# Products without a reader on TensorE, ahead of the first queries and beside the 24 leading maxima

## The chip, the cores and the metric

The kernel runs on one core of one Trainium2 chip. The metric is the time of one execution on the device in microseconds (us), median of the runs; a profiled execution gives the trace that the views are read from. Its span runs from the first to the last instruction, so it is a little shorter than the time.

## The reference, cut to what matters

Two transformer layers over `x` of shape (4, 512, 128). Each normalizes `x`, and adds attention with 16 heads of 8 dimensions and a feed-forward part, both taken from the same normalized `x`:

```python
xn = _layernorm(x)
x = x + _L0_attn_ref(xn, ...) + _L0_ffn_ref(xn, ...)
xn = _layernorm(x)
x = x + _L1_attn_ref(xn, ...) + _L1_ffn_ref(xn, ...)   # block mask; 8 experts, top 2
...
scores = jnp.einsum('bhqd,bhkd->bhqk', q, k) / math.sqrt(HEAD_DIM)
attn = jax.nn.softmax(scores, axis=-1)                 # needs the largest score of each row
out = jnp.einsum('bhqk,bhkd->bhqd', attn, v)
```

The change touches neither inputs nor outputs of any of this.

## The kernel before

The work is cut into eight units (`U = 8`), one for each layer and sequence. A unit has 32 pairs of heads and query tiles for the maxima and 16 slots for the rest of the attention. The order on each engine is written out by hand in five programs, one for each engine, which meet at semaphores.

**The start.** SyncE loads `xs` and the first weights. VectorE takes the statistics, GpSimd the deviation, VectorE normalizes (`normalize`, L521). TensorE turns the result over in `xnT_mms` (four f32 transposes, L729), ScalarE copies it to SBUF (`xnT_copy`, L1003), and TensorE makes queries and keys in `qk_mm` (L735: w_q and w_k, f32, 512 columns; a product is two instructions in the trace) and values in `v_mms` (L741). ScalarE copies with bias (L1020) and, with VectorE, splits each value into three bf16 parts (L1008, L573, L1013, L577). SyncE writes the parts to DRAM (`z`, L422) and reads them back in the layout of the operands `QO` and `KO` (L443).

**The leading maxima.** Ahead of unit 0, 24 pairs of its maxima are made (`LEAD = 24`). `max_mms` (L777) issues two bf16 products of 48 rows by 512 columns for each pair; one works on partitions 0 to 47, the other on 64 to 111. They fill one of three pairs of PSUM banks (banks 0 to 5), and `read_max` on VectorE (L1194) reduces 1,024 columns to the maxima. `take_pair` makes a pair of banks wait for the read that last used it, three jobs back in a list `taken`. After 20 pairs stand four small transposes (`max_transposes`, L784), of which ScalarE makes `mT` (L1027), and two DMAs put it into rows of `QO` (L470).

**The slots.** In `tensor_unit` each slot has two pairs of score products (L792), two pairs of maxima for later (L777), eight instructions of `value_mms` (L808, f32, into bank 6, `PV_BANK`), and side work. ScalarE takes the exponential of each score pair (L1034).

Bank 6 is used at the start for the queries of unit 0 and then for the bias of the values (`value_bias`, L755), which VectorE reads in `add_value_bias` (L1183), with `v_bias_added` as its signal. After that nobody touches it until `value_mms` of slot 0.

Of the kernel before, what the change touches and what calls it, by code (L numbers as in the profile page):

```python
# [12 lines left out]
P = 128  # L13
# [4 lines left out]
def build(nc, x, wq, wk, wv, bq, bk, bv, wo, bo, wg_T, wu_T, wd_T, src_blocks, tgt_blocks, router_T, eg_T, eu_T,  # L18
# [3 lines left out]
    NT = S // P  # L22
# [19 lines left out]
    PROD_ROWS, MASK_ROW, M_ROW, ROWS = 48, 48, 56, 59  # L42
# [9 lines left out]
    with ExitStack() as ctx:  # L52
        def sb(name, shape, dt=F32):
            return ctx.enter_context(nc.sbuf_tensor(name, shape, dt))

        def sem(name):
            return ctx.enter_context(nc.semaphore(name))

        ident = sb("ident", [P, P])
# [44 lines left out]
        QO = [sb(f"QO{i}", [P, H // 2, S], BF16) for i in range(3)]  # L104
        KO = [sb(f"KO{i}", [P, H // 2, S], BF16) for i in range(3)]
# [50 lines left out]
        ps = ctx.enter_context(nc.psum_tensor("ps", [P, 8, 512], F32))  # L156
# [5 lines left out]
        PV_BANK, SIDE = 6, 7  # L162
# [23 lines left out]
        v_bias_added = sem("v_bias_added")  # L186
# [72 lines left out]
        def layer(u):  # L259
            return u // B  # L260
# [12 lines left out]
        def rows_of(t, half, j, rows, blocks):  # L273

            return t[64 * half:64 * half + rows, j, blocks[0] * P:blocks[1] * P]

        def reads_of(u):

            return 16 * sum(4 if layer(v) == 0 else 16 for v in range(u % 3, u + 1, 3))

        def late_reads_of(u):

            return 16 * 16 * sum(layer(v) == 1 for v in range(u % 3, u + 1, 3))
# [50 lines left out]
        def take_pair(pe, kind, n):  # L334

            i = turn[kind, n]
            if i >= 3:
                before, m = taken[i - 3]
                left = {"score": exp_done, "max": max_read, "gate0": h_ready[0], "gate1": h_ready[1],
                        "places": places_ready, "expert": y_copied}[before]  # L340
                pe.wait_ge(left, m + 1)
            return i % 3
# [383 lines left out]
        def xnT_mms(pe, p, bank):  # L726
            pe.wait_ge(xn_ready, p + 1)
            for t in range(NT):
                last = pe.transpose(ps[:, bank, t * P:(t + 1) * P], xe[p % 2][:, t, 0, 0:D], ident[:])  # L729
            last.then_inc(xnT_ps, 1)  # L730

        def qk_mm(pe, p, side, bank):
            pe.wait_ge(xnT_ready, p + 1)
            w = (w_q, w_k)[side][layer(p)]
            pe.matmul(ps[:, bank, :], w[:], xnT[p % 4][:], start=True, stop=True).then_inc(qk_ps, 1)  # L735

        def v_mms(pe, p, bank):
            if layer(p) == 0:
                for t in range(NT):
                    tok = slice(t * P, (t + 1) * P)  # L740
                    last = pe.matmul(ps[:, bank, tok], xnT[p % 4][:, tok], w_v[0][:], start=True, stop=True)  # L741
            else:

                for h in range(H):
                    for c4 in range(4):
                        last = pe.matmul(ps[32 * c4:32 * c4 + 32, bank, 32 * h:32 * h + 32],
                                         xnT[p % 4][:, 32 * h:32 * h + 32], w_v[1][:, 32 * c4:32 * c4 + 32],
                                         start=True, stop=True)
            last.then_inc(v_ps, 1)

        def value_bias(pe):

            pe.wait_ge(proj_loaded, 16 * 3)
            pe.wait_ge(part_ready[0], 1)
            pe.matmul(ps[:, PV_BANK, 0:D], b_v0[:].to_broadcast([P, P]), w_proj[0][:], start=True, stop=True).then_inc(  # L755
                v_bias_ps, 1)

        def max_mms(pe, q):
            u, m = q // PAIRS_U, q % PAIRS_U
            s, qt, jj = m // 8, m % 8 // 2, m % 2  # L760
            if m == 0:
                if u == 0:
                    pe.wait_ge(first_rows[0], 16 * 4)
                else:
                    pe.wait_ge(qk_rows[u % 3], reads_of(u))
                if B <= u < B + 3:
                    pe.wait_ge(mask_rows, 32 * (u - B + 1))
            if q == PAIRS_U // 4:
                pe.wait_ge(first_rows[1], 16 * 4)
            if q == PAIRS_U // 2:  # L770
                pe.wait_ge(qk_rows[0], reads_of(0))
            if m == PAIRS_U // 2 and layer(u) == 1:
                pe.wait_ge(late_rows[u % 3], late_reads_of(u))
            pair = take_pair(pe, "max", q)
            rows = PROD_ROWS if layer(u) == 0 else M_ROW
            for half in range(2):
                mm = pe.matmul(ps[:, 2 * pair + half, :], rows_of(QO[u % 3], half, 2 * s + jj, rows, (qt, qt + 1)),  # L777
                               rows_of(KO[u % 3], half, 2 * s + jj, rows, (0, NT)), start=True, stop=True)
            mm.then_inc(max_ps, 1)

        def max_transposes(pe, u, a):
            pe.wait_ge(m_split, 2 * u + a + 1)
            for t in range(NT):
                last = pe.transpose(ps_bf(SIDE)[0:24, t * P:(t + 1) * P],  # L784
                                    mp[:, a, t].rearrange("p h i j -> p (h i j)"), ident_bf[:])
            last.then_inc(mT_ps, 1)
# [103 lines left out]
        def side_mms(pe, u, slot):  # L890

            w, n, p, f = u - 1, u + 1, u + 2, u + 3
            if slot == 0 and 1 <= u and p < U:
                pe.wait_ge(mT_ready, 2 * u + 1)
                pe.wait_ge(h_ready[0], GATES_U * min(u, B))
                qk_mm(pe, p, 0, SIDE)
# [8 lines left out]
            if slot == 2 and u == 0:  # L905
                qk_mm(pe, p, 0, SIDE)
            if slot == 3 and u >= 1:
                normalized_transposes(pe, w)
            if slot == 4 and p < U:
                pe.wait_ge(qk_f_ready, 2 * p + 1)  # L910
                pe.wait_ge(onT_ready, u)
                qk_mm(pe, p, 1, SIDE)
# [75 lines left out]
        def last_tensor(pe):  # L988
            u = U - 1
            value_mms(pe, SLOTS_U * U - 1)  # L990
            pe.wait_ge(on_ready, 2 * u + 1)
            out_transposes(pe, u, 1)
            normalized_transposes(pe, u)

            out_mms(pe, u, (0, 1), PV_BANK)
            pe.wait_ge(onT_ready, u + 2)
            out_mms(pe, u, (2, 3), PV_BANK)
# [432 lines left out]
        @block.sync  # L1430
        def _(sp):
            load_x(sp, 0)
            for dst, src in first_loads:
                sp.dma_start(dst, src).then_inc(first_loaded, 16)
            load_x(sp, 1)
            load_x(sp, 2)
            for dst, src in proj_loads:
                sp.dma_start(dst, src).then_inc(proj_loaded, 16)
            operand_writes(sp, 0, 0)
            operand_writes(sp, 0, 1)  # L1440
            first_reads(sp)
            row_constants(sp, 0)
            for dst, src in ffn_loads:
                sp.dma_start(dst, src).then_inc(ffn_loaded, 16)
            operand_writes(sp, 1, 0)
            operand_writes(sp, 1, 1)
            operand_reads_0(sp, 1)
            max_rows(sp, 0, 0)
            row_constants(sp, 1)
            row_constants(sp, 2)  # L1450
            load_x(sp, 3)
            for dst, src in loads:
                sp.dma_start(dst, src).then_inc(loaded, 16)
            for u in range(U):
                sync_unit(sp, u)
            for b in ARRIVALS:
                load_results(sp, b)
            for b in ARRIVALS:
                store(sp, b)
            sp.wait_ge(stored, 16 * B)  # L1460
# [65 lines left out]
        @block.tensor  # L1526
        def _(pe):
            pe.wait_ge(consts, N_IDENT)
            xnT_mms(pe, 0, SIDE)
            pe.wait_ge(first_ready, 1)  # L1530
            qk_mm(pe, 0, 0, PV_BANK)
            qk_mm(pe, 0, 1, 4)
            v_mms(pe, 0, 5)
            xnT_mms(pe, 1, SIDE)
            qk_mm(pe, 1, 0, SIDE)
            pe.wait_ge(qk_f_ready, 3)
            qk_mm(pe, 1, 1, SIDE)
            value_bias(pe)
            pe.wait_ge(v_read, 1)
            pe.wait_ge(part_ready[1], 1)  # L1540
            for q in range(20):
                max_mms(pe, q)
            pe.wait_ge(qk_f_ready, 4)
            max_transposes(pe, 0, 0)
            for q in range(20, LEAD):
                max_mms(pe, q)
            pe.wait_ge(v_bias_added, 1)
            pe.wait_ge(mT_ready, 1)
            for u in range(U):
                tensor_unit(pe, u)  # L1550
            last_tensor(pe)
# [51 lines left out]
```

## Time and profile before

| what | value |
|---|---|
| median of 3 runs | 523.88 us (523.43 to 524.0) |
| the profiled execution | 523.32 us, span 521.1 us |
| PE busy | 454.9 us, 87% |
| DVE busy | 396.2 us, 76% |
| ACT busy | 331.9 us, 64% |
| POOL busy | 266.5 us, 51% |
| mean granted clock of TensorE | 0.957 |

A busy share is a mean over stages that have different limits. PEclk is the granted clock: 1.00 is 2.4 GHz and 0.50 is 1.2 GHz. It changes twice in the first 60 us, so that stretch is read by itself. The last two rows of the stretches (from 507.6 us on) show the same thing at the end of the kernel.

### The profile page before, as it was taken

The page shows a single profiled execution, that of the slowest core. Times are in us where ns is not written, and L with a number is a line of the kernel's source. Part 1 is how long each engine was busy: PE and PEld are TensorE (multiplying, and loading weights), DVE is VectorE, ACT ScalarE, POOL GpSimd, SP SyncE. Part 2 cuts the span into 40 slices and gives each one's busy share as a digit, 9 for nine tenths or more (in the row PEclk, how much of TensorE's full clock was granted, in tenths as well). Part 3 has the DMA queues.
Part 4 walks back from the last instruction along what each step waited for, and adds up shares of the span by engine and source line. Part 5 has one row for each costly group of instructions (what it writes and reads, how often), then busy time and mean ns, then how long its engine had stood idle before and what let it go on. Part 6 is the DMA issues. An engine that isn't in the chain of part 4 may idle for free.

```text
span 521.1 us, 9480 instructions
## 1 busy us (share of the span) xinstructions
PE 454.9 (87%) x3442; PEld 177.3 (34%) x3442; DVE 396.2 (76%) x554; ACT 331.9 (64%) x439; POOL 266.5 (51%) x503
## 2 busy tenths in 40 slices
PE   3555989999999999999999988987999999999962
PEld 1201223324432443243424222221245453555512
DVE  3499889996999699969996988888886777723304
ACT  2301677776677677757776777767766657577570
POOL 6782085724535473787388758874202233163434
PEclk9855899999999999999999999999999999999995
DMA  3797439534820361636162636355721111010025
GB/s 86 223 237 109 75 115 269 152 147 150 175 87 20 124 62 20 64 124 87 20 67 81 119 40 64 120 92 70 97 55 36 42 54 50 2 48 20 31 82 189
DMA packets 140734, 48.27 MB, mean 93 GB/s; under 512 B 109954, under 2 KB 135058, under 8 KB 139858
## 3 DMA queue, kind: packets, MB, share of 16 engines
q1 hardware_dynamic: 138386, 42.93, 39.3%
q0 software_dynamic: 2304, 4.76, 2.7%
q8 instruction: 27, 0.44, 0.4%
q14 instruction: 17, 0.14, 0.1%
HBM read 22.81 MB, written 23.14 MB: 88 GB/s over the span
## 4 chain that ended last, share of the span: by engine, by line
PE 59%; DVE 17%; ACT 9%; issue 8%; DMA 3%; POOL 2%; SPq 1%; ACTq 0%; DVEq 0%; POOLq 0%
PE ps L808 16%; DVE mx L1194 11%; PE ps L792 10%; PE ps L777 8%; ACT PT L1034 6%; PE ps L849 3%; PE ps L735 3%; PE ps L857 3%; PE ps L832 3%; PE ps L850 2%; PE ps L872 2%; PE ps L833 2%; PE ps L869 2%; PE ps L816 1%; POOL y_tokens L550 1%
## 5 line engine op out<-in xcount | busy, mean ns | idle before, releaser
L1194 DVE TENSOR_REDUCE mx<-ps 128x2 f32<-128x1024 f32 x256 | 307.6, 1220 | 57.6 <-PE ps L777 54.2
L1034 ACT ACTIVATE PT<-ps 128x1024 f32<-128x1024 f32 x256 | 258.6, 1025 | 107.6 <-PE ps L792 101.7
L808 PE MATMUL ps<-PT,Vp 128*32 128x512 f32 x1024 | 137.9, 608 | 4.5 <-ACT PT L1034 4.4
L777 PE MATMUL ps<-KO,QO 48*128 48x512 bf16 (+1 forms) x512 | 103.9, 403 | 32.1 <-ACT PT L1034 15.9
L792 PE MATMUL ps<-QO,KO 59*128 59x512 bf16 x512 | 99.9, 388 | 1.3 <-DVE mx L1194 1.1
L550 POOL DMA_INDIRECT y_tokens<-expert_io,meta x40 | 38.4, 961 | 67.5 <-ACT expert_io L1069 50.2
L792 PEld LDWEIGHTS ps<-QO,KO 59*128 59x128 bf16 x512 | 24.5, 93 | 137.2 <-issue 74.9
L1216 DVE SCALAR_TENSOR_TENSOR th<-th,ps 128x320 f32<-128x320 f32 (+1 forms) x56 | 25.5, 455 | 31.9 <-ACT th L1054 31.6
L777 PEld LDWEIGHTS ps<-KO,QO 48*128 48x128 bf16 (+1 forms) x512 | 25.6, 96 | 61.7 <-ACT PT L1034 28.8
L538 POOL DMA_INDIRECT x_places<-xe,place_i x32 | 31.8, 993 | 20.0 <-ACT PT L1034 14.4
L587 POOL CAST mp<-mx 128x32 bf16<-128x32 f32 x16 | 3.4, 211 | 71.9 <-DVE mx L1194 67.9
L808 PEld LDWEIGHTS ps<-PT,Vp 128*32 128x32 f32 x1024 | 20.3, 108 | 46.2 <-issue 40.3
L1054 ACT ACTIVATE th<-ps 128x320 f32<-128x320 f32 (+1 forms) x56 | 23.1, 418 | 11.9 <-PE ps L849 6.5
L1232 DVE SCALAR_TENSOR_TENSOR h_all<-th,ps 128x320 f32<-128x320 f32 (+1 forms) x56 | 25.7, 458 | 1.9
L849 PE MATMUL ps<-expert_io,eg 128*128 128x320 f32 x64 | 24.4, 463 | 1.5 <-DVE h_all L1232 0.5
L1027 ACT COPY mT<-ps 24x512 bf16<-24x512 bf16 x16 | 9.0, 560 | 25.2 <-PE ps L784 25.2
L1069 ACT ACTIVATE expert_io<-ps,meta 128x128 f32<-128x128 f32 x40 | 11.2, 371 | 18.0 <-PE ps L857 18.0
L850 PE MATMUL ps<-expert_io,eu 128*128 128x320 f32 x64 | 22.5, 432 | 0.0
L521 POOL TENSOR_SCALAR xe<-xs,mv,rstd 128x128 f32<-128x128 f32 x28 | 22.0, 792 | 0.8
L857 PE MATMUL ps<-ed,h_all 128*128 128x128 f32 x160 | 19.4, 276 | 1.2 <-DVE h_all L1232 1.2
L857 PEld LDWEIGHTS ps<-ed,h_all 128*128 128x128 f32 x160 | 18.9, 192 | 3.0 <-DVE h_all L1232 1.7
L1200 DVE RECIPROCAL rden<-ps 128x32 f32<-128x32 f32 x16 | 5.6, 348 | 15.9 <-PE ps L816 15.9
(168 smaller groups left out, 491.3 us busy)
## 6 DMA issues: line engine op xcount, KB each, us to landing
z<-part SPq DMA_DIRECT2D x16, 384.0 KB, 2.6
z<-part SPq DMA_DIRECT2D x16, 256.0 KB, 3.0
QO<-z SPq DMA_DIRECT2D x64, 48.0 KB, 2.7
KO<-z SPq DMA_DIRECT2D x64, 48.0 KB, 2.6
x_places<-expert_io SPq DMA_DIRECT2D x2, 1300.0 KB, 7.2
expert_io<-x_places SPq DMA_DIRECT2D x8, 320.0 KB, 3.7
QO<-z SPq DMA_DIRECT2D x6, 384.0 KB
KO<-z SPq DMA_DIRECT2D x6, 384.0 KB
```

Of the source, the lines that this page charges most:

```text
L538: pool.indirect_dma_start(out=x_places[:], out_offset=bass.IndirectOffsetOnAxis(ap=place_i[:, b, t, k:k + 1], axis=0), in_=xe[p % 2][:, t, ...
L550: pool.indirect_dma_start(out=y_tokens[:], out_offset=bass.IndirectOffsetOnAxis(ap=meta[:].bitcast(I32)[:, e, j, 0:1], axis=0), in_=y_sb[e ...
L777: mm = pe.matmul(ps[:, 2 * pair + half, :], rows_of(QO[u % 3], half, 2 * s + jj, rows, (qt, qt + 1)), rows_of(KO[u % 3], half, 2 * s + jj, ...
L792: mm = pe.matmul(ps[:, 2 * pair + half, :], rows_of(KO[u % 3], half, 2 * s + jj, ROWS, (k, k + 1)), rows_of(QO[u % 3], half, 2 * s + jj, R ...
L808: last = pe.matmul(ps[32 * g:32 * g + 32, PV_BANK, :], Vp[u % 2][:, k, head(s, g), :], PT[:, (2 * t + g % 2) % 4, g // 2, :], start=(s % 2 ...
L849: pe.matmul(ps[:, 2 * pair, 0:HALF], eg[:, e, cols], x_T, start=True, stop=True).then_inc(gate_ps[1], 1)
L850: pe.matmul(ps[:, 2 * pair + 1, 0:HALF], eu[:, e, cols], x_T, start=True, stop=True).then_inc(up_ps[1], 1)
L857: last = pe.matmul(across(pair, j * P, (j + 1) * P), h1_T[:, e % 2, i, j * P:(j + 1) * P], ed[:, e, i, :], start=(i == 0), stop=(i == EB - 1))
L1034: act.activation(PT[:, e % 4], ps[:, 2 * pair:2 * pair + 2, :], ACT.Exp).then_inc(exp_done, 1)
L1194: dve.tensor_reduce(mx[:, a, qt, col:col + 5:4], ps[:, 2 * pair:2 * pair + 2, :], AX_X, ALU.max, negate=True).then_inc(max_read, 1)
L1216: dve.scalar_tensor_tensor(out=t, in0=t, scalar=1.0, in1=gate, op0=ALU.add, op1=ALU.mult).then_inc(gate_done[L], 1)
L1232: dve.scalar_tensor_tensor(out=dst, in0=t, scalar=0.5, in1=up, op0=ALU.mult, op1=ALU.mult).then_inc(h_ready[L], 1)
```

## The change

Two helpers are added. `clock_mms` multiplies the identity by itself into bank 0, n times: 18 times ahead of `xnT_mms` of unit 0 and twice behind it. `clock_mm` repeats the first product of the pair of maxima just issued (partitions 0 to 47) into bank 6, once for each of the 24 leading pairs. No instruction reads what they write, and they signal nothing. The wait for `v_bias_added`, which stood behind the leading maxima, now stands ahead of the first `clock_mm`, that is behind the first pair of maxima.

```diff
+        def clock_mms(pe, n):
+
+            for _ in range(n):
+                pe.transpose(ps[:, 0, 0:P], ident[:], ident[:])
+
...
+
+        def clock_mm(pe, q):
+
+            if q == 0:
+                pe.wait_ge(v_bias_added, 1)
+            s, qt, jj = q // 8, q % 8 // 2, q % 2
+            pe.matmul(ps[:, PV_BANK, :], rows_of(QO[0], 0, 2 * s + jj, PROD_ROWS, (qt, qt + 1)),
+                      rows_of(KO[0], 0, 2 * s + jj, PROD_ROWS, (0, NT)), start=True, stop=True)
...
             pe.wait_ge(consts, N_IDENT)
+            clock_mms(pe, 18)
             xnT_mms(pe, 0, SIDE)
+            clock_mms(pe, 2)
             pe.wait_ge(first_ready, 1)
...
             for q in range(20):
                 max_mms(pe, q)
+                clock_mm(pe, q)
             pe.wait_ge(qk_f_ready, 4)
             max_transposes(pe, 0, 0)
             for q in range(20, LEAD):
                 max_mms(pe, q)
-            pe.wait_ge(v_bias_added, 1)
+                clock_mm(pe, q)
             pe.wait_ge(mT_ready, 1)
```

On TensorE the start of the program, up to the first two pairs of maxima, was this before:

```order
1 L729 MATMUL ps<-ident,xe 128x128 [waits xn_ready,consts]
2 L729 MATMUL ps<-ident,xe 128x128 x3
3 L735 MATMUL ps<-xnT,w_q 128x512 [waits xnT_ready,first_ready]
4 L735 MATMUL ps<-xnT,w_k 128x512 [waits xnT_ready]
5 L741 MATMUL ps<-w_v,xnT 128x128 x4
```

With the change, on the same engine at the same place (line numbers are those of the changed kernel, in which L740 is the former L735):

```order
1 L735 MATMUL ps<-ident 128x128 [waits consts]
2 L735 MATMUL ps<-ident 128x128 x17
3 L729 MATMUL ps<-ident,xe 128x128 [waits xn_ready]
4 L729 MATMUL ps<-ident,xe 128x128 x3
5 L735 MATMUL ps<-ident 128x128 x2
6 L740 MATMUL ps<-xnT,w_q 128x512 [waits xnT_ready,first_ready]
7 L740 MATMUL ps<-xnT,w_k 128x512 [waits xnT_ready]
```

Eighteen products now stand ahead of the first transposes and wait for the identity alone, and two stand between those transposes and the first query product. Further down TensorE's program, the leading maxima and the first slots stood so before:

```order
9 L777 MATMUL ps<-KO,QO 128x512 x40
10 L784 MATMUL ps<-ident_bf,mp 24x128 x4
11 L777 MATMUL ps<-KO,QO 128x512 x8
12 L792 MATMUL ps<-QO,KO 128x512 x2
13 L777 MATMUL ps<-KO,QO 128x512 x2
```

With the change, the end of that stretch reads as follows (L782 and L805 are the former L777 and L792, and L791 is the added product):

```order
49 L782 MATMUL ps<-KO,QO 128x512 x2
50 L791 MATMUL ps<-KO,QO 128x512
51 L797 MATMUL ps<-ident_bf,mp 24x128 x4
52 L782 MATMUL ps<-KO,QO 128x512 x2
53 L791 MATMUL ps<-KO,QO 128x512
...
58 L782 MATMUL ps<-KO,QO 128x512 x2
59 L791 MATMUL ps<-KO,QO 128x512
60 L805 MATMUL ps<-QO,KO 128x512 x2
61 L782 MATMUL ps<-KO,QO 128x512 x2
```

One product has come in behind each pair of maxima, and none behind the pairs of maxima inside the slots.

## Rows read from the trace of the kernel before

**Rows 1.** The page: the share of each engine in the chain that ended last.
```profile
PE 59%; DVE 17%; ACT 9%; issue 8%; DMA 3%; POOL 2%; SPq 1%; ACTq 0%; DVEq 0%; POOLq 0%
```

**Rows 2.** The stretches: busy time of each engine, PEclk, DMA share, GB/s.
```profile
core 0: us, PE busy (x) PEld busy (x) DVE busy (x) ACT busy (x) POOL busy (x), PEclk, DMA share, GB/s
15.70:20.00 4.30, 2.72 (x8) 0.97 (x6) 2.97 (x12) 1.87 (x4) 1.25 (x2) 1.00 0.84 276
20.00:22.50 2.50, 0.00 (x0) 0.00 (x0) 0.29 (x1) 0.50 (x1) 2.36 (x4) 1.00 0.74 195
22.60:24.50 1.90, 0.00 (x1) 0.03 (x1) 0.00 (x0) 0.00 (x0) 1.76 (x3) 0.50 0.87 247
24.50:50.20 25.70, 14.75 (x52) 2.88 (x52) 25.05 (x23) 0.57 (x1) 14.88 (x22) 0.50 0.84 184
53.60:56.70 3.10, 3.10 (x14) 0.51 (x16) 2.37 (x2) 1.54 (x2) 0.00 (x0) 0.50 0.50 62
56.70:60.10 3.40, 3.40 (x25) 1.01 (x23) 2.45 (x2) 2.74 (x4) 0.00 (x0) 1.00 0.65 97
...
500.00:507.60 7.60, 4.68 (x38) 0.80 (x34) 0.00 (x0) 4.90 (x5) 2.87 (x3) 1.00 0.32 103
507.60:510.60 3.00, 1.23 (x12) 0.84 (x8) 1.12 (x4) 0.58 (x1) 2.26 (x2) 1.00 1.03 335
510.70:521.10 10.40, 2.09 (x9) 1.78 (x8) 4.59 (x5) 1.03 (x2) 3.32 (x3) 0.50 0.49 152
```

**Rows 3.** The chain that ended last, in order of time: start us, us, what.
```profile
7.85 1.10 PE ps L729 x4
8.97 0.59 ACT xnT L1003
...
9.70 3.77 PE ps L735 x4
...
25.15 28.38 DVE mx L1194 x25
...
53.58 0.60 PE ps L792
```

**Rows 4.** The timeline: start us, us, engine, line, operands, and the idle time before.
```profile
2.02 0.29 POOL L1325 TENSOR_SCALAR_AFFINE_SELECT ident_bf<-ident_bf 128x128 bf16<-128x128 bf16 x1
20.03 0.29 DVE L1183 TENSOR_TENSOR b_proj<-ps,b_proj 128x128 f32<-128x128 f32 x1 [1.24 <-PE ps L755]
24.50 1.46 PE L777 MATMUL ps<-KO,QO 48*128 48x512 bf16 x6 [4.50 <-DMA KO<-z]
26.43 0.61 PE L777 MATMUL ps<-KO,QO 48*128 48x512 bf16 x2 [0.47 <-DVE mx L1194]
45.06 0.60 PE L784 MATMUL ps<-ident_bf,mp 128*24 128x128 bf16 x4
50.27 0.61 PE L792 MATMUL ps<-QO,KO 59*128 59x512 bf16 x2 [0.61 <-DVE mx L1194]
54.71 1.93 PE L808 MATMUL ps<-PT,Vp 128*32 128x512 f32 x8
58.13 0.39 PE L777 MATMUL ps<-KO,QO 48*128 48x512 bf16 x2
58.45 1.06 PE L808 MATMUL ps<-PT,Vp 128*32 128x512 f32 x8
61.58 1.06 PE L808 MATMUL ps<-PT,Vp 128*32 128x512 f32 x8
```

**Rows 5.** Queries' products: those started from 9 to 16 us, then those from 16 to 20.
```profile
L735 PE MATMUL ps<-xnT,w_q x2: 1061/1127/1193, 9.7 to 10.7; 128*128 128x512 f32 x2
...
L735 PE MATMUL ps<-xnT,w_q x2: 592/644/697, 16.7 to 17.3; 128*128 128x512 f32 x2
```

**Rows 6.** Reads of the maxima from 24 to 53 us, then from 60 to 110.
```profile
L1194 DVE TENSOR_REDUCE mx<-ps x25: 1211/1212/1225, 25.1 to 52.3; 128x2 f32<-128x1024 f32 x25
...
L1194 DVE TENSOR_REDUCE mx<-ps x32: 1193/1225/1227, 60.1 to 108.7; 128x2 f32<-128x1024 f32 x32
```

## The prediction

> **What bounds the kernel now.** I read the page first: PE holds 59% of the chain that ended last, DVE 17% [rows 1]. Then the chain in order of time, since the change lies within the first 50 us. Up to 24.5 us it is a string of single steps: transposes, a copy, the products of queries and keys [rows 3], then casts, a write to DRAM and a read back. From 25.15 to 53.53 us it is VectorE alone: 25 reads of the maxima, 28.38 us, one each 1.135 us [rows 3]. From 53.58 us on it is TensorE's products, nearly unbroken.
>
> Then I read the stretches for TensorE's granted clock. It is 1.00 (2.4 GHz) until 22.5 us, 0.50 (1.2 GHz) from there to 56.7, and 1.00 again until 510.6 [rows 2]. The column must not be trusted before 15.7 us: it says full speed, but a product of the queries took 1,061 to 1,193 ns at 9.7 us and 592 to 697 ns at 16.7 us, with the same operands [rows 5]. So TensorE starts at its lower level too. What it did before each move: it rose during unbroken work from 9.7 us on and again from 53.6 to 56.7 (3.10 us busy of 3.10). It fell after 2.5 us of no work at 22.5, and near 510.6 after a stretch in which it was busy 1.23 us of 3.00. It stayed high with 2.72 us of 4.30 at 15.7 to 20 and with 4.68 of 7.60 at 500 to 507.6. It stayed low through the leading maxima with 14.75 of 25.70 [rows 2].
>
> The low clock costs nothing while VectorE is the bound (24.5 to 53.5 us). It costs in two places: in the products at the start of the chain, and from 53.58 to 56.7 us, where TensorE is the bound and still slow.
>
> **The 20 transposes of the identity.** The identities are ready at 2.31 us [rows 4]. Four transposes took 1.10 us at the low level [rows 3]; with some 0.42 us for the last to end, that is one each 0.22 us, so 18 take 4.2 us and end at 6.5. The first real transposes start at 7.85, so 1.3 us of idle time hides the 18. Without overlap between neighbours, at 0.42 us each, they would end at 9.9 us and cost 2.0; the four rows in 1.10 us exclude that. The other two take 0.4 us in the 0.75 us between 8.95 and 9.70, hidden by ScalarE's copy of 0.59.
>
> What they give: were the clock high from 7.85 us on, the query and key products (3.77 us) would take about 2.0 (starts that were 0.85 to 0.99 apart halve, and the last takes 0.59 [rows 5]), and the transposes 0.66 instead of 1.10 by the same ratio. That is 2.2 us off the chain, the upper bound; the lower is nothing. I take 0.5, nearer the lower: if the clock has risen by 6.5 us, TensorE then has only six transposes in the 3.2 us up to 9.7, which is like the stretch ahead of 510.6 us in which it fell. A part remains, because the two products behind `xnT_mms` make the work from 7.85 on nearly unbroken, so that the rise should come 1 to 2 us sooner and fall within the key product.
>
> The Trainium skill ("TensorE: Matmul & The Clock Gate", Part 4: PE-mode transpose) says that full clock does not engage for transposes, as they don't count as TensorE being busy in the same way. By that rule this term is 0 and the sum is 0.5 us smaller; the trace doesn't decide it, as its rise near 15.7 us followed products and transposes together.
>
> **The 24 products beside the maxima.** Pairs at the low level start 0.43 us apart when nothing holds them: three took 1.46 us, one alone 0.61 [rows 4]. The added product uses the partitions of the first of the two, so it comes behind it: 0.43 us more for each pair, 1.04 us in a period of 1.135, hidden by VectorE's read. Behind the first pairs it adds up to 0.43 x 2 = 0.9 us: pair 3 ends near 27.7, and VectorE wants it at 25.15 + 3 x 1.135 = 28.55. The four transposes for `mT` come 0.43 us later (45.5 instead of 45.06), and so do the copy and the two DMAs; slot 0's wait at 50.27 us was ended by a read of maxima [rows 4], so the DMAs had landed by then. Its cost is 0 to 0.43 us; I take 0. The moved wait costs nothing: the value bias was added at 20.03 us, before the maxima began [rows 4], and only the added products stand behind it.
>
> What they give: from 24.5 us TensorE is busy without a break for about 5 us (the first pairs with their additions, at the low level), as long as the stretches after which it rose, so I expect the rise by 29.6 us. At the high level a pair takes 0.39 us [rows 4] and the addition half of 0.43, 0.60 us of 1.135, or 53%. The rows show a fall at 41% (1.23 of 3.00) and none at 62% (4.68 of 7.60) and 63% (2.72 of 4.30). That 53% holds is therefore the weak step. If it does, the clock is high at 50.27 us. VectorE's pace stays, and what shrinks is 53.58 to 56.7 us: 3.12 us of TensorE's work take half, 1.56. As a control: eight value products took 1.93 us there and 1.06 later, and the distance between groups of them was 3.74 us against 3.13 next [rows 4], with the score product ahead of the first 0.2 us shorter. The bounds are 0 and 1.8; I take 1.5. The work behind it is one chain of TensorE, so the gain is carried to the end.
>
> **The sum.** 0.5 + 1.5 = 2.0 us, so the profiled execution's 523.32 becomes 521.3. The median was 0.56 us above it. The rise at 56.7 us came 3.1 us after unbroken work began, the one at the start only after some 6; executions in which it comes later lose more in both places, and a high clock through the maxima takes that away. So I take another 0.3 from the median: 523.88 - 2.0 - 0.3 = 521.6.
>
> **Rivals.** *The clock doesn't hold in the maxima* (26%). It rises near 29 us and falls again at 53% busy, and TensorE meets slot 0 at the low level. Against it stand the 62% and 63% rows; for it, the fall at 41%. Only the start gives something: 523.88 - 0.5 = 523.4, 522.9 to 523.9. *Nothing moves the clock* (13%): identity products don't count, by the page's rule above, and three products of 48 rows in a period are as little as the two that left it low for 25.7 us. The time is 523.9. *VectorE reads slower* (9%): the products write PSUM while VectorE reads it, and VectorE is the bound for 25 reads. Reads took 1,212 ns beside the sparse low-level products and 1,225 beside the dense ones after 60 us [rows 6], so 0.013 x 25 = 0.3 us is what the rows bear out. It decides from 2.0/25 = 0.08 us a read; at 0.14 us, the time would be 523.88 - 2.0 + 3.5 = 525.4.
>
> **How the numbers follow.** My case has 52%, and its own range is 519.9 (the start's full 2.2 us and 1.8) to 522.6 (no gain at the start, 1.3 at the maxima). About 0.2%, or 1.05 us, can be told from no change. Faster by more: my case and the best part of the first rival, 0.55. Within it: most of the first two, 0.36. Slower: the third, 0.09. The range goes from 519.9 to 524.3 and leaves out the slow rival and little else.
>
> **What would show it.** Rows of the query products at 9.7 us under 1,000 ns show the first gain, and the first maxima then start before 24.0. PEclk 1.00 from some point before 30 us to 50 us and beyond shows the second; 0.50 in the stretch of 45 to 53 refutes it. The 25 reads must still take 28.4 us; over 29 would show the third rival. The first value products should take 1.06 us and start before 54.4, counted from the first read at 25.15. The prediction is wrong on the low side if the start is at full clock throughout, and on the high side if 53% busy is too little.

## Result, and the profile after

The changed kernel takes 525.38 us (median of 22 runs, 522.68 to 527.19), the kernel before 523.83 (22 runs beside it, 522.41 to 524.84). The ratio is 1.0027, with a 95% interval of 1.0015 to 1.004: slower by 1.5 us, where 521.6 was forecast. The profiled execution took 525.33 us.

Lines have moved: L735 is now L740, L777 is L782, L792 is L805, L808 is L821, L746 is L751, L1034 is L1047, L1194 is L1207. The page of the changed kernel says (span, granted clock in 40 slices, an instruction queue, chain by engine); the last line, the scores' products with their idle time, is from the list of TensorE's groups:

```profile
span 523.0 us, 9567 instructions
PEclk9655999999999999998999999999999999999985
q8 instruction: 28, 0.46, 0.4%
PE 63%; DVE 15%; ACT 11%; issue 8%; DMA 2%; POOL 0%; SPq 0%; ACTq 0%; DVEq 0%
L805 PE MATMUL ps<-QO,KO 59*128 59x512 bf16 x512 | 100.5, 391 | 3.1 <-issue 2.3 <-DVE mx L1207 0.7
```

VectorE's share of the chain fell from 17% to 15% and TensorE's rose from 59% to 63% [rows 1]. Two marks point at the place of the loss, neither near the added instructions: PEclk has an 8 in the nineteenth slice (235 to 248 us), and 2.3 us of idle time ahead of L805 were ended by nothing that the profile knows ("issue"). The page of before counts 27 instruction packets in q8, this one 28.

**The start gained.** The chain that ended last, in order of time (start us, us, what):

```profile
7.56 0.67 PE ps L729 x4
8.26 0.59 ACT xnT L1016
8.85 0.14 issue
8.99 1.11 PE ps L740 x2
...
22.00 0.63 PE ps L782 x2
22.64 28.39 DVE mx L1207 x25
```

Transposes take 0.67 us instead of 1.10, two query products 1.11 from 8.99 on, and the first read stands at 22.64 us instead of 25.15 [rows 3]: 2.5 us earlier. The 25 reads take 28.39 us, as before. (A second trace of the kernel before, `before_again`, has its first read at 24.34; the size of this gain is taken up again below.)

**The lead gained nothing.** Stretches (busy time and count of each engine, PEclk, DMA share, GB/s), and the timeline around the first slots:

```profile
core 0: us, PE busy (x) PEld busy (x) DVE busy (x) ACT busy (x) POOL busy (x), PEclk, DMA share, GB/s
22.00:27.20 5.20, 5.20 (x18) 1.54 (x18) 4.55 (x5) 0.00 (x0) 4.79 (x7) 0.50 0.78 175
27.20:50.00 22.80, 20.14 (x65) 3.04 (x66) 22.80 (x22) 1.60 (x2) 11.61 (x18) 0.50 0.83 177
50.00:54.40 4.40, 4.30 (x18) 0.62 (x20) 3.47 (x3) 2.05 (x2) 0.00 (x0) 0.50 0.50 61
54.50:58.00 3.50, 3.50 (x25) 1.18 (x22) 2.73 (x3) 3.02 (x4) 0.00 (x0) 1.00 0.67 103
239.00:242.10 3.10, 3.10 (x14) 0.33 (x12) 2.27 (x9) 1.29 (x2) 3.02 (x5) 0.50 0.76 77
```
```profile
52.21 1.93 PE L821 MATMUL ps<-PT,Vp 128*32 128x512 f32 x8
...
56.08 1.06 PE L821 MATMUL ps<-PT,Vp 128*32 128x512 f32 x8
```

TensorE is busy for all of the 5.2 us after the maxima begin and for 88% of the 22.8 behind them, and the clock stays at 0.50. The first value group takes 1.93 us as before, and the next starts 3.87 us behind it instead of 3.74 [rows 4].

**The loss lies at 235 us.** I compared ScalarE's 256 exponentials of both traces one by one. The changed kernel is 2.4 us ahead from 58 us to 235 us and 1.0 behind from 243 us on, and up to 504 us nothing else moves it by more than 0.7. So 3.4 us are lost at one place. TensorE's timeline there, of the kernel before and then of the changed one:

```profile
237.32 1.58 PE L746 MATMUL ps<-w_v,xnT 128*32 128x32 f32 x128
238.83 0.39 PE L792 MATMUL ps<-QO,KO 59*128 59x512 bf16 x2
239.06 0.38 PE L777 MATMUL ps<-KO,QO 56*128 56x512 bf16 x2
239.37 1.06 PE L808 MATMUL ps<-PT,Vp 128*32 128x512 f32 x8
```
```profile
234.95 1.30 PE L751 MATMUL ps<-w_v,xnT 128*32 128x32 f32 x128
238.52 0.40 PE L805 MATMUL ps<-QO,KO 59*128 59x512 bf16 x2 [2.27 <-issue]
238.75 0.60 PE L782 MATMUL ps<-KO,QO 56*128 56x512 bf16 x2
239.28 1.93 PE L821 MATMUL ps<-PT,Vp 128*32 128x512 f32 x8
```

The burst makes the values of layer 1's first unit: 128 products of 32 columns with weights of 32 columns, each with a weight load, so 256 instructions in 1.3 us. Before, the next product follows at once. Now TensorE stands for 2.27 us with nothing to wait for, and then the clock is 0.50 from 238.78 to 242.19 us (window 239.00 to 242.10 above; the value group takes 1.93 instead of 1.06). The idle time and the low clock together are the 3.4 us.

What differs ahead of it is work that nobody waits for, and the count of instructions. I put all of TensorE's instructions in the trace (products, weight loads, semaphore instructions) in the order of their starts: 7,086 before, 7,173 after. The 87 more are 44 products and their 44 loads, less one semaphore instruction, since the wait for the identity now rides on a product. The burst is instructions 2,666 to 2,921 before and 2,753 to 3,008 after. All waits of 0.9 to 2.3 us that end by nothing known, up to 500 us and in all sixteen traces of this case, stand at 3,009 or 4,801, both 193 above a multiple of 256. (Shorter ones, of 0.3 to 0.6 us, stand elsewhere too, in the traces of the first chip.) An instruction packet of the DMA queues is 16,384 bytes, 64 for each of 256 instructions. So the theory: TensorE is handed its program in blocks of 256 instructions, the next one is fetched while one runs, and where the burst falls exactly on one block, it is used up in 1.3 us and TensorE stands until the next has come. The Trainium skill ("Runtime: NRT & Kernel Launch", Instruction fetch mechanics) has the same blocks and calls the cost of crossing one "mostly hidden"; at this crossing 2.27 us of it were not.

The trace also shows the fetch. The kernel before has 27 packets in q8 and 27 block ends (193, 449, and so on up to 6,849), the changed one 28 and 28. Between 235.9 and 237.3 us the view of DMA queues has one of them (packets, MB, share of the 16 engines), and none from 235 to 235.9 or from 237.3 to 238.6:

```profile
q8 instruction: 1, 0.02, 5.6%
```

By its record the packet begins at 235.96 us, 1.01 behind the block's first instruction, and ends at 237.22. The next instruction starts at 238.52, 1.30 behind the packet's end.

The rival: the wait comes from the kind of the added work (writes to bank 6, a moved wait, power drawn earlier), not from its count.

### The profile page after: what moved, and what is told of

Its sections match the earlier page's. It is cut to its first block, busy times and chain, and to the rows that moved or that the text cites. A ratio compares the mean times of both kernels' runs of the same rounds, so it can differ in the third digit from the quotient of the medians.

```text
span 523.0 us, 9567 instructions
## 1 busy us (share of the span) xinstructions
PE 470.6 (90%) x3486; PEld 182.0 (35%) x3486; DVE 396.8 (76%) x554; ACT 331.9 (63%) x439; POOL 267.6 (51%) x503
## 4 chain that ended last, share of the span: by engine, by line
PE 63%; DVE 15%; ACT 11%; issue 8%; DMA 2%; POOL 0%; SPq 0%; ACTq 0%; DVEq 0%
PE ps L821 18%; PE ps L805 11%; DVE mx L1207 10%; PE ps L782 8%; ACT PT L1047 7%; PE ps L870 4%; PE ps L862 3%; PE ps L845 3%; PE ps L740 3%; PE ps L863 2%; PE ps L885 2%; PE ps L846 2%; PE ps L882 2%; PE ps L829 2%; ACT qk_f L1033 1%
## 5 line engine op out<-in xcount | busy, mean ns | idle before, releaser
L1207 DVE TENSOR_REDUCE mx<-ps 128x2 f32<-128x1024 f32 x256 | 307.7, 1222 | 57.7 <-PE ps L782 54.5
L1047 ACT ACTIVATE PT<-ps 128x1024 f32<-128x1024 f32 x256 | 258.6, 1025 | 111.6 <-PE ps L805 105.9
L821 PE MATMUL ps<-PT,Vp 128*32 128x512 f32 x1024 | 139.9, 619 | 4.5 <-ACT PT L1047 4.4
L782 PE MATMUL ps<-KO,QO 48*128 48x512 bf16 (+1 forms) x512 | 105.6, 406 | 20.4 <-ACT PT L1047 15.9
L805 PE MATMUL ps<-QO,KO 59*128 59x512 bf16 x512 | 100.5, 391 | 3.1 <-issue 2.3
L805 PEld LDWEIGHTS ps<-QO,KO 59*128 59x128 bf16 x512 | 24.5, 93 | 141.2 <-issue 77.5
L782 PEld LDWEIGHTS ps<-KO,QO 48*128 48x128 bf16 (+1 forms) x512 | 26.0, 96 | 56.1 <-ACT PT L1047 28.7
L821 PEld LDWEIGHTS ps<-PT,Vp 128*32 128x32 f32 x1024 | 20.3, 109 | 46.1 <-issue 40.0
L521 POOL TENSOR_SCALAR xe<-xs,mv,rstd 128x128 f32<-128x128 f32 x28 | 23.1, 835 | 3.4 <-DMA x_places<-xe,place_i 2.9
```

The costliest lines, as they stand in the source:

```text
L805: mm = pe.matmul(ps[:, 2 * pair + half, :], rows_of(KO[u % 3], half, 2 * s + jj, ROWS, (k, k + 1)), rows_of(QO[u % 3], half, 2 * s + jj, R ...
L821: last = pe.matmul(ps[32 * g:32 * g + 32, PV_BANK, :], Vp[u % 2][:, k, head(s, g), :], PT[:, (2 * t + g % 2) % 4, g // 2, :], start=(s % 2 ...
L1047: act.activation(PT[:, e % 4], ps[:, 2 * pair:2 * pair + 2, :], ACT.Exp).then_inc(exp_done, 1)
L1207: dve.tensor_reduce(mx[:, a, qt, col:col + 5:4], ps[:, 2 * pair:2 * pair + 2, :], AX_X, ALU.max, negate=True).then_inc(max_read, 1)
```

## Experiments

They ran on several chips; each ratio is against the kernel before on the same chip. On the first chip (`start_only`, `lead_only`, `after_again`, `shift_44`) that took 527.48 us, on the others 523.7 to 523.8.

### One half each: `start_only` and `lead_only`

```diff
+            clock_mms(pe, 18)             # start_only: these two alone
             xnT_mms(pe, 0, SIDE)
+            clock_mms(pe, 2)
...
                 max_mms(pe, q)
+                clock_mm(pe, q)           # lead_only: these alone, with the moved wait
```

> The change's 20 identity transposes alone, without the 24 products beside the maxima. Theory A (the late loss is TensorE's supply of instructions: 128 value products of the fifth unit begin just where a block of its program ends, because 87 instructions came in ahead of them): here only 40 came in, the burst begins elsewhere in its block, so no wait of over 1 us behind it near 236 us, and the start's gain of about 2.4 us is kept: 521.0 to 522.0. Theory B (the work runs 2.4 us earlier and meets other DMA traffic): the start is as early, so the wait of 2.3 us comes all the same: about 525.

> The change's 24 products beside the maxima alone, without the 20 transposes. They kept the clock low in the changed kernel, so by every theory the stretch up to 60 us takes what it took before (first score product 50.3 us, low clock until 54 to 57). Theory A: 47 instructions are ahead of the burst instead of 87, no wait over 1 us behind it, 523.4 to 524.4. Theory B: nothing is earlier, so no wait either, same time. A third view, that the products themselves hurt VectorE's reads: the 25 reads take over 29 us and the time is over 525.

Measured: `start_only` 0.9965 (0.9947 to 0.9983), `lead_only` 0.9984 (0.9965 to 1.0003), while the whole change, run again beside them as `after_again`, is at 1.0043. Halves that cost nothing alone make a loss together: that is no property of either kind of work. Neither trace has a wait behind the burst (the next product starts 0.13 us after its last in both; by the traces 39 and 48 instructions more put the block's end elsewhere). Both have a wait of 0.35 and 0.31 us inside it, behind its 35th product, which is no block's end. In `start_only` the clock can be followed by itself, since only transposes have run:

```profile
2.37 3.79 PE L735 MATMUL ps<-ident 128*128 128x128 f32 x18 [2.37 <-POOL ident_bf L1338]
7.81 0.66 PE L729 MATMUL ps<-ident,xe 128*128 128x128 f32 x4 [1.66 <-DVE xe L521]
8.30 0.38 PE L735 MATMUL ps<-ident 128*128 128x128 f32 x2
9.23 2.05 PE L740 MATMUL ps<-xnT,w_q 128*128 128x512 f32 x2 [0.55 <-ACT xnT L1016]
```

The clock rose at 5.70 us, within the 18 transposes, and fell again at 9.11 us, ahead of the query products, after 1.23 us busy of the 3.20 from 5.80 to 9.00. In the changed kernel it rose at 6.67 us and held until 16.91. `lead_16`, further down, has the very same instructions up to there and fell as `start_only` did (up at 5.59, down at 9.00). `lead_only` had TensorE busy 24.30 us of 26.00 in the maxima at 0.50.

> The changed kernel once more, for a second trace. Theories A and B: a wait of TensorE of over 1.5 us without a releaser behind the 128 value products near 236 us again. Chance: no such wait in this execution. The clock at the start rises before 10 us by both; through the leading maxima it stays low if products of 48 rows count for little, and is high in some executions if it is a matter of when the burst falls.

It lost again, with a shorter wait at the block's end and no fall of the clock there:

```profile
234.87 0.53 PE L751 MATMUL ps<-w_v,xnT 128*32 128x32 f32 x36
235.77 1.03 PE L751 MATMUL ps<-w_v,xnT 128*32 128x32 f32 x92 [0.38 <-issue]
237.74 0.39 PE L805 MATMUL ps<-QO,KO 59*128 59x512 bf16 x2 [0.94 <-DVE mx L1207]
```

The releaser named in the last line is a read of maxima that had long ended; the wait sits at the same instruction, 3,009, 1.45 us behind its packet's end. The 0.38 us behind the 36th product are like the pause that `start_only` and `lead_only` have, so they don't belong to the block's end.

### The count without the work: `shift_44`

The kernel before, with 44 products of 8 columns with weights of 32 columns, in idle time at 2.37 us. They take 1.33 us, and no later instruction reads what they write. They are 88 instructions, and here too one semaphore instruction falls away: 87 more by the trace, the change's own number.

```diff
+        def tiny_mms(pe, n):
+            for _ in range(n):
+                pe.matmul(ps[0:32, 0, 0:8], ident_bf[:, 0:32], ident_bf[:, 0:8], start=True, stop=True)
...
             pe.wait_ge(consts, N_IDENT)
+            tiny_mms(pe, 44)
             xnT_mms(pe, 0, SIDE)
```

> The kernel before with 44 very small products (32 columns of weights, 8 moving columns, no reader) in TensorE's idle time ahead of the first transposes: 88 more instructions ahead of everything, as in the change, and no work to speak of. Theory A: a wait of 2 to 2.5 us comes behind the 128 value products near 239 us, often with a fall of the clock, and the time is 2.5 to 4 us over the kernel before: 526 to 528. Theory B and chance: the time of the kernel before, 523.4 to 524.4.

Measured: 1.0049 (1.003 to 1.0068), 530.41 against 527.48 us. The real transposes took 1.12 us as before, so it gained nothing at the start, and the wait is back, at instruction 3,009:

```profile
237.39 0.50 PE L751 MATMUL ps<-w_v,xnT 128*32 128x32 f32 x35
238.22 1.42 PE L751 MATMUL ps<-w_v,xnT 128*32 128x32 f32 x93 [0.33 <-issue]
240.80 0.39 PE L797 MATMUL ps<-QO,KO 59*128 59x512 bf16 x2 [1.16 <-issue]
```

The count alone makes a loss, without any of the change's work. The rival falls. The medians are 2.9 us apart; the exponentials of this trace fall behind those of `lead_only`, on the same chip, by 1.4 us at this burst. What makes the rest was not followed up.

### The work with another count: `pad_151` and `pad_256`, beside `before_again`

The changed kernel with tiny products added: 32 behind the 18 transposes (151 instructions over before), and 52 more ahead of the first maxima (255).

```diff
             clock_mms(pe, 18)
+            tiny_mms(pe, 32)
...
+            tiny_mms(pe, 52)              # pad_256 only, ahead of the leading maxima
             for q in range(20):
```

> The changed kernel with 32 very small products more between the 18 transposes and the first real ones, hidden in idle time: 151 instructions ahead of the bursts of 128 value products instead of 87. Theory A (a wait at the end of a block of 256 instructions, when the burst runs through the block before it faster than the next arrives): the block that ends at instruction 3009 now ends 192 instructions into the first burst, and the one that ends at 4033 ends 236 into the second. TensorE waits at both, 0.5 to 2 us each, inside the bursts and no longer behind the first: the time is that of the changed kernel or up to 2 us more, 0 to +6 us against the kernel before. Theory B (the early start meets other traffic): one wait behind the first burst, as in the changed kernel.

> The changed kernel with 84 very small products more (32 behind the 18 transposes, 52 in the idle time ahead of the first maxima): 255 instructions ahead instead of 87, so that every burst stands in its block as in the kernel before, to one instruction. The work starts as early as in the changed kernel. Theory A: no wait behind the first burst, and what the start gives is kept: 2 to 3 us faster than the kernel before. Theory B: the wait of 1 to 2.5 us near 236 us is there, and the time is 1.5 to 2.5 us over the kernel before.

> The kernel before once more, for a trace on this chip. All theories: no wait of over 1 us without a releaser behind the 128 value products near 237 us; the clock goes low near 22 us and high between 54 and 60 us. It is the base for the traces of the same chip.

Measured: `pad_151` 522.12 us, 0.9962 (0.9947 to 0.9977); `pad_256` 522.15 us, 0.9965 (0.9952 to 0.9979). More instructions made the changed kernel 3 us faster than it was without them. No wait stands behind the burst in either:

```profile
234.99 1.45 PE L756 MATMUL ps<-w_v,xnT 128*32 128x32 f32 x128
236.37 0.39 PE L810 MATMUL ps<-QO,KO 59*128 59x512 bf16 x2
```

In `pad_151` I had expected waits within bursts, and there were none. At the first burst a block that holds 64 instructions of ordinary work beside part of the burst lasts 5.62 us, longer than a block takes to come. At the second the block lasts 2.69 us and it was just in time: the packet ended 1.27 us ahead of the block that it brings.

`before_again` (one execution, 524.2 us) shows that the kernel before pays too: its block ends behind the third burst, and eight value products are split by a wait of 0.50 us at instruction 4,801. `pad_151` starts 2.5 us ahead of it and is 3.9 ahead behind that burst; `pad_256`, whose clock rose only at 11.57 us, starts 1.0 ahead and is 2.4 ahead there.

### How much of a block must be fast: `pad_103` and `lead_16`

```diff
+            tiny_mms(pe, 8)               # pad_103: the changed kernel and these (103)
...
+                if q < 16:                # lead_16: added products beside 16 pairs only (71)
+                    clock_mm(pe, q)
```

> The changed kernel with 8 very small products more behind the 18 transposes: 103 instructions ahead of the bursts instead of 87. The block that ends at instruction 3009 then ends 240 instructions into the first burst, and the block before it 16 ahead of the burst. Theory A: those 16 give the fetch only some 0.5 to 1 us more, so a wait of 0.3 to 1.5 us is left at instruction 3009, inside the burst; the time lies between the changed kernel's (1.5 to 2.3 us over before) and that with 151 (1.6 us under before). Theory B has no reason for a difference from the changed kernel.

> The changed kernel with a product beside the first 16 pairs of maxima only: 71 instructions ahead instead of 87, the start as in the changed kernel. The first burst ends 16 instructions ahead of the end of its block at 3009, which are then ordinary work of some 1 us. Theory A: the wait at instruction 3009 is 1 us shorter than in the changed kernel, 0 to 1.3 us, and no longer directly behind the burst; the time is 0.5 to 1.5 us under that of the changed kernel. Theory B: as the changed kernel.

`pad_103`: 523.0 us, 0.9989 (0.9977 to 1.0), between the changed kernel and `pad_151` as expected, but without the expected wait at 3,009; at 4,033, a block's end behind the next burst, it has a gap of 0.5 us, start to start, that ends 1.43 us behind the packet's end. `lead_16`: 523.99 us, 1.0005 (0.9992 to 1.0018). In `lead_16` the burst ends 16 instructions ahead of its block's end, and the wait moves by just these, into the value group. A second one, longer, stands at 4,801, inside the third burst:

```profile
238.57 1.05 PE L821 MATMUL ps<-PT,Vp 128*32 128x512 f32 x3
239.95 1.05 PE L821 MATMUL ps<-PT,Vp 128*32 128x512 f32 x5 [0.33 <-issue]
```

The time that TensorE needs for instructions 2,753 to 3,008, the gap ahead of 3,009 (start to start), and how long before 3,009 the packet ended that brings it:

| kernel | more than before | block runs in us | gap at its end, us | from the packet's end, us |
|---|---|---|---|---|
| after | 87 | 1.10 | 2.46 | 1.30 |
| after_again | 87 | 1.74 | 1.14 | 1.45 |
| shift_44 | 87 | 2.06 | 1.35 | 1.32 |
| lead_16 | 71 | 2.45 | 0.92 | 1.32 |
| pad_103 | 103 | 2.83 | 0.00 | 1.42 |
| lead_only | 48 | 4.25 | 0.00 | 1.95 |
| start_only | 39 | 5.30 | 0.21 | 3.02 |
| pad_151 | 151 | 5.62 | 0.00 | 5.22 |
| before | 0 | 7.20 | 0.06 | 4.81 |

In the four with a wait, block and gap add up to 2.9 to 3.6 us at this burst, but that is no constant. At 5,825 of the changed kernel the sum is 1.9 us (1.50 and 0.39), and at 4,801 of `lead_16` a block of 4.78 us was followed by a gap of 1.31. What varies is when the packet begins, 0.46 us ahead of the block's first instruction in the one case and 3.58 behind it in the other. What doesn't vary is the last column: over all block ends of the sixteen traces no block begins sooner than 1.24 us behind its packet's end, and the six gaps of 0.9 us and more named so far (four above, 4,801 of `lead_16` and of `before_again`) end 1.30 to 1.61 us behind it. TensorE waits for the packet.

### Why the clock stayed low: `wide_256`, `fill_narrow`, `fill_wide`

All three carry tiny products, so that the first burst doesn't fill one block. `wide_256` is `pad_256` with each added product made 128 rows high. `fill_wide` has two such products for each pair (512 and 256 columns), `fill_narrow` the same two with the old 48 rows.

```diff
-            pe.matmul(ps[:, PV_BANK, :], rows_of(QO[0], 0, 2 * s + jj, PROD_ROWS, (qt, qt + 1)),
-                      rows_of(KO[0], 0, 2 * s + jj, PROD_ROWS, (0, NT)), start=True, stop=True)
+            for n in (NT, 2):             # wide_256: NT alone; fill_narrow: the old operands
+                pe.matmul(ps[:, PV_BANK, 0:n * P], ident_bf[:],
+                          ident_bf[:].unsqueeze(1).to_broadcast([P, n, P]), start=True, stop=True)
```

> As the padded kernel with 84 small products, but each of the 24 products beside the maxima multiplies the bf16 identity over all 128 rows by 512 columns, instead of 48 rows. Same count of instructions, same columns. Theory R (rows count: products of 48 rows do little to raise the clock, so that it stayed low through the maxima though TensorE was busy 97 to 99% for 3 to 6 us): the clock rises before 31 us, is high at 50 us if three products in 1.13 us hold it, and the stretch from the first score product to the second group of value products is 1 to 1.7 us shorter: 1 to 1.7 us faster than the padded kernel. Theory N (the low clock in the maxima has another cause, as the free 0.27 us in each period): it stays low until 54 us or later and the time is the padded kernel's.

> The same with 48 rows instead of 128 in both added products, and the same 151 instructions. If rows count (products of 48 rows, even two side by side, leave most of the array idle), the clock stays low through the maxima: low until 54 us, 1.5 to 2.5 us faster than before. If only time counts, it rises here as with all rows.

> Beside each of the 24 pairs of maxima stand two products of the bf16 identity over all 128 rows, with 512 and 256 columns, so that TensorE is busy 1.07 us of each 1.135 at the low clock; 8 very small products behind the 18 transposes bring the count of instructions ahead of the bursts to 151, at which no wait at a block's end was seen. Theory F (it takes unbroken work over all rows): the clock rises within 7 us of the first maxima; then three products of 0.21, 0.21 and 0.11 us stand in each 1.135 us, and if that holds it, the clock is high at 50 us and the kernel is 3 to 4 us faster than before. Theory L (nothing in this stretch raises it): low until 54 us or later, 1.5 to 2.5 us faster than before.

Measured: 522.42 us, 0.9968 (0.9953 to 0.9983); 522.26 us, 0.9968 (0.9957 to 0.9979); 522.63 us, 0.999 (0.9973 to 1.0006). The stretches of the leading maxima, of `wide_256`, of `fill_narrow`, of `fill_wide`:

```profile
24.00:50.00 26.00, 26.00 (x76) 5.22 (x74) 25.53 (x23) 0.57 (x1) 14.80 (x22) 0.50 0.89 187
```
```profile
24.00:48.00 24.00, 24.00 (x93) 10.86 (x92) 24.00 (x22) 0.57 (x1) 15.97 (x23) 0.50 0.82 180
```
```profile
24.00:30.80 6.80, 6.80 (x24) 1.27 (x22) 6.46 (x6) 0.00 (x0) 6.54 (x9) 0.50 0.74 159
30.90:51.30 20.40, 15.26 (x80) 4.03 (x78) 20.40 (x19) 1.87 (x3) 7.94 (x14) 1.00 0.79 164
51.40:54.70 3.30, 2.97 (x14) 0.54 (x16) 2.63 (x3) 1.68 (x2) 0.00 (x0) 0.50 0.48 57
```

With 48 rows TensorE was busy for every microsecond from 24 to 48 and stayed at 1.2 GHz. With 128 rows and the same columns it went to 2.4 GHz at 30.88 us. This is no accident of one execution: the mean granted clock was 0.962 to 0.979 in the 12 executions of `fill_wide` and 0.938 to 0.954 in the 11 of `fill_narrow`. So busy time is the wrong measure: what the products are counts too, by this pair of kernels their rows (their operands also differ in content, the identity instead of queries and keys). One full-height product for each pair was too little. And `fill_wide` gained nothing in the end: until the rise its pairs came 1.29 us apart and held VectorE's reads (25 reads from the first to the last start took 28.14 us instead of 27.16), and the clock fell at 51.36 us, in slot 0, where it had no additions.

### The best of it: `hold_wide`, beside `start_151`

`hold_wide` is `fill_wide` with three more pairs of additions in slot 0 and 2 tiny products instead of 8 (151 instructions). `start_151` keeps only the 20 transposes and fills up to some 150 with 55 tiny products.

```diff
+                if u == 0 and slot == 0:  # at three places of slot 0, behind products of scores or maxima
+                    clock_mm(pe, 1)
```

> As the kernel with two products of the identity over 128 rows (512 and 256 columns) beside each leading pair, with three more such pairs of products in the idle time of slot 0, so that the clock, high from about 31 us, needs not fall before slot 1; again 151 instructions ahead of the bursts. If my term holds: the clock is high from 31 us on without a fall, the first group of value products takes 1.06 us instead of 1.93, and from the first read of the maxima to the second group of value products it is 1.2 to 1.7 us shorter than in the kernels with a low clock there. The reads are held up somewhat while the clock is low, 0.15 us each for some 8 pairs, so the time is 2 to 3 us under the kernel before. Rival: VectorE's reads, not TensorE, set slot 0 and 1, and the shortening is under 0.5 us.

> The 20 identity transposes and very small products in idle time up to 151 instructions, with no product beside the leading maxima. If the 24 products of 48 rows do nothing (the clock stays low with and without them, VectorE's reads hide them), the time is that of the kernel with them and 151 instructions, 1.3 to 2.3 us under the kernel before. If they cost by delaying mT or give by an earlier rise behind 53 us, it differs by up to 0.5 us.

`hold_wide`: 521.44 us, 0.9956 (0.994 to 0.9973), faster than both kernels. `start_151`: 522.35 us, 0.9972 (0.996 to 0.9985). The stretch of `hold_wide` between 24.2 and 50 us and its first two value groups, then those of `start_151`:

```profile
24.20:50.00 25.80, 20.02 (x104) 5.33 (x102) 25.80 (x24) 1.60 (x2) 15.42 (x23) 1.00 0.82 170
```
```profile
51.42 1.06 PE L826 MATMUL ps<-PT,Vp 128*32 128x512 f32 x8
54.25 1.07 PE L826 MATMUL ps<-PT,Vp 128*32 128x512 f32 x8
```
```profile
52.49 1.88 PE L826 MATMUL ps<-PT,Vp 128*32 128x512 f32 x8
56.14 1.06 PE L826 MATMUL ps<-PT,Vp 128*32 128x512 f32 x8
```

The clock rose at 24.12 us, soon enough that the reads lost little, and held until 501.98. That it rose so soon is luck of the execution, since `fill_wide` has the same work up to slot 0 but for six tiny products and rose at 30.88. From the first read to the second value group it is 32.13 us, in `start_151` 33.21, in all fourteen traces with a low clock there 33.03 to 34.30. Against `before_again` the exponentials from 62 us on come 4.40 us earlier in `hold_wide` and 2.51 in `start_151`. But 0.81 of these 1.9 us lie ahead of the first read (22.12 and 22.93), where the two kernels differ by tiny products alone. So a clock that is held is worth 1.1 us by these two traces. The medians are 0.9 us apart, with intervals that overlap.

## Why the prediction was wrong

**The step that failed** is one that it did not have: that products in idle time or beside VectorE cost nothing, because "the work behind it is one chain of TensorE, so the gain is carried to the end". The instructions are also a count, which moved 87 places under the rest of the program. At 235 us a burst of 256 short instructions came to lie on one block, and 2.27 us of idle time and the low clock behind it cost 3.4 us. The prediction had put the additions at nothing beyond the time that they take. `shift_44` shows the count as cause, `pad_151` and `pad_256` take the loss away with the work in place, and the packet's record shows what TensorE waits for. The range, 519.9 to 524.3, had no room for it: its one slow rival was about VectorE's reads, which took 28.39 us, so that its 525.4 us meets the measured 525.38 by chance. Without the wait the change measures 522.1 us (`pad_151`, `pad_256`) where 521.6 was forecast, and that is luck too, for the two terms of the sum came out otherwise.

**The start: 0.5 us forecast, 2.5 measured**, above even the bound of 2.2. The mechanism was right: the clock rose within the 18 transposes or soon behind them, in ten traces of twelve. The size differs from one execution to the next. The first read stands at 24.25 to 25.15 us in the four traces without these transposes, so 0.8 of the 2.5 are the late trace of before. It stands at 22.12 to 22.93 in the eight with them where the clock rose at 6.40 to 7.26 us and held beyond 13.8, and at 23.83 to 24.47 in the other four: the clock fell again at 9.0 and 9.1 us (`lead_16`, `start_only`), much as I had forecast, or rose only at 11.5 (`pad_256`, `wide_256`). Some 0.3 us of the 2.5 are an earlier `xe` (7.56 against 7.85), which the change does not touch.

**The maxima: 1.5 us forecast, -0.1 measured** (0.9 against `before_again`, whose clock rose later, at 58.48 us). I named the holding of the clock at 53% busy as the weak step, but it failed one step earlier: the clock did not rise. I had taken "busy without a break for 5 us" as enough. It was so in the rows, where most of the work had 128 rows, but not for 48 rows, even at 100% (`fill_narrow`). The size itself was fair: where the clock is held (`hold_wide`) it is worth 1.1 us against `start_151`, and 0.9 to 2.2 against all traces with a low clock.

**The Trainium skill's rule** ("TensorE: Matmul & The Clock Gate", Part 4: PE-mode transpose), by which transposes don't engage the full clock: `start_only` has the rise at 5.70 us after f32 transposes alone, and the next four take 0.66 us. Here they do, though not each time: in `pad_256` the same 18 took 4.10 us and the next four still 1.12.

**The rivals.** "Nothing moves the clock" was half right: the products of 48 rows did not. "VectorE reads slower" was refuted. The sum of this trace: -2.5 at the start, 0.1 at the maxima and 3.4 at the burst give +1.0, and ScalarE's exponentials were 1.0 us behind. The rest to the 1.9 of the span arises after 504 us; the clock fell at 505.02 us there and at 510.68 before.

**Open.** The profiled executions of most padded kernels are 1 to 2 us faster than their medians (`start_151` 520.31 against 522.35, `pad_151` 521.06 against 522.12), that of before is 0.6 us faster. What their other executions pay no trace shows; a late packet at another burst would do it and is only a guess. What sets when a packet begins is open too. That other transfers of the same DMA engines hold it up is a guess: at 235 us the packet and a burst of transfers coincide, but no run changed that.

## What to carry to other kernels

Instructions put into idle time aren't free in a kernel with bursts of very short instructions: count how many stand ahead of the burst, look for idle time that ends by "issue" far behind the change, and hold it against the packets of the instruction queue. If a small change moves the time oddly, add a few tiny products at an idle place and see if it goes away. If you fill idle time to raise TensorE's clock, the products of full height did it here and those of 48 rows did not; begin ahead of the work that needs it, and go on until dense work takes over.

## What the runs showed that I had not expected

- A block of 256 TensorE instructions begins no sooner than 1.24 us behind the end of its 16 KB packet. Where a block ran in 1.1 to 2.5 us, that left gaps of up to 2.46 us, start to start; a packet that began late (3.58 us into its block) left 1.31 behind a block of 4.78.
- 2.3 us of idle time at full clock were followed by a fall to 1.2 GHz in one execution and 0.94 us were not in another.
- TensorE busy for 24.00 us of 24.00 with 48-row products stays at 1.2 GHz; with added products of 128 rows and the same columns it rises.
- With eighteen f32 transposes of the identity at 2.37 us the clock was up by 5.59 to 7.26 us in ten traces of twelve and at 11.5 in two; without them it rose at 13.88 to 15.75. The column PEclk shows 1.00 from the start of the trace all the same.
